# Which tiles of a softmax sum VectorE adds, and where the maxima stand: one edit to an attention kernel

## The reference, cut to what matters

```
h = layernorm(x) * (1 + ca) + sa                       # 2 x 2048 x 256
q, k, v = split_heads(h @ W + b)                       # 16 heads of 64
pattern = einsum('bhid,bhjd->bhij', k, q) / sqrt(64)
prob = softmax(pattern, axis=-2)                       # over the 2048 rows i
out = einsum('bhis,bhid->bhsd', prob, v)
x = x + ga * (concat(out) @ Wo + bo)
```

## Time and profile before

| | |
|---|---|
| Median of 3 runs | 4717.73 us (4717.35 to 4722.87) |
| Profiled execution, its own time | 4722.76 us |
| Span in the trace | 4721.0 us |
| PE busy | 4368.3 us (93%) |
| DVE busy | 3253.8 us (69%) |
| POOL busy | 2907.6 us (62%) |
| ACT busy | 2169.1 us (46%) |
| Chain that ended last, by engine | POOL 53%, issue 21%, PE 12%, DVE 8%, ACT 4% |

### The profile page before, as it was taken

How to read it: one execution, slowest core, us unless ns; L and a number is a source line. 1 busy time by engine, 2 the same in 40 slices (tenths; PEclk the granted TensorE clock), 3 DMA queues, 4 the chain that set the end, 5 groups by cost and what they waited for, 6 DMA issues and landing times.

```text
span 4721.0 us, 67306 instructions
## 1 busy us (share of the span) xinstructions
PE 4368.3 (93%) x25496; PEld 2574.1 (55%) x25496; DVE 3253.8 (69%) x4370; ACT 2169.1 (46%) x3523; POOL 2907.6 (62%) x1269
## 2 busy tenths in 40 slices
PE   7999999999999999999999999759998896989898
PEld 5545454454454454554545544337676675767575
DVE  6777877878777877778777787455654545665455
ACT  5444444444444444444444444326565434556442
POOL 2867767667667677677676676526665334666332
PEclk8999999999999999999999999879999998999899
DMA  2000000000000000000000000100000000000001
GB/s 78 6 11 14 7 11 7 14 11 5 15 11 5 11 15 6 11 13 8 11 6 15 11 5 7 40 18 1 1 1 5 33 1 19 1 1 1 1 1 36
DMA packets 81402, 55.74 MB, mean 12 GB/s; under 512 B 48532, under 2 KB 71016, under 8 KB 81128
## 3 DMA queue, kind: packets, MB, share of 16 engines
q1 hardware_dynamic: 81128, 51.92, 4.1%
HBM read 30.66 MB, written 4.19 MB: 7 GB/s over the span
## 4 chain that ended last, share of the span: by engine, by line
POOL 53%; issue 21%; PE 12%; DVE 8%; ACT 4%; POOLq 1%; DMA 0%; DVEq 0%; SPq 0%; ACTq 0%
POOL accp L770 41%; POOL lp L792 4%; PE psum L1665 4%; POOL accp L766 3%; PE psum L1794 2%; POOL rnorm L782 2%; POOL qk_u L787 2%; PE psum L1807 2%; DVE ssq L1262 1%; ACT lp L974 1%; PE psum L1711 1%; ACT qk_sq L958 1%; DVE qk_w L1274 1%; POOL ug_l L820 1%; DVE lneg L1288 1%
## 5 line engine op out<-in xcount | busy, mean ns | idle before, releaser
L770 POOL TENSOR_TENSOR accp<-accp,prob 128x1024 f32<-128x1024 f32 x704 | 1766.9, 2510 | 492.5 <-ACT prob L928 414.0
L928 ACT ACTIVATE prob<-psum 128x1024 f32<-128x1024 f32 x1024 | 1020.0, 1024 | 1461.4 <-PE psum L1518 1383.6
L1159 DVE TENSOR_REDUCE mx<-psum 128x1 f32<-128x512 f32 x1984 | 1276.2, 684 | 347.2 <-PE psum L1485 298.0
L1530 PE MATMUL psum<-prob,vv 128*64 128x512 f32 x4096 | 993.2, 606 | 0.0
L1485 PE MATMUL psum<-kh,qh 64*128 64x512 f32 x2048 | 493.6, 471 | 56.1 <-DVE mx L1159 48.7
L1530 PEld LDWEIGHTS psum<-prob,vv 128*64 128x64 f32 x4096 | 248.7, 136 | 490.3 <-issue 427.3
L1485 PEld LDWEIGHTS psum<-kh,qh 64*128 64x128 f32 x2048 | 205.3, 185 | 522.6 <-DVE mx L1159 442.0
L792 POOL TENSOR_TENSOR lp<-lp,lrcp 128x1024 f32<-128x1024 f32 x128 | 297.9, 2327 | 238.0 <-DVE lrcp L1294 238.0
L1518 PE MATMUL psum<-nm,one 64*128 64x512 f32 x2048 | 428.7, 408 | 13.9 <-ACT prob L928 6.5
L1518 PE MATMUL psum<-qh,kh 64*128 64x512 f32 x2048 | 412.2, 391 | 0.0
L1518 PE MATMUL psum<-qh,kl 64*128 64x512 f32 x2048 | 412.1, 391 | 0.0
(11 more groups left out here) (197 smaller groups left out, 6942.3 us busy)
## 6 DMA issues: line engine op xcount, KB each, us to landing
kl<-kl SPq DMA_DIRECT2D x64, 256.0 KB, 3.8
wqk<-L_attn_Wq SPq DMA_DIRECT2D x64, 64.0 KB, 2.0
rot_l<-const_rot SPq DMA_DIRECT2D x2, 2048.0 KB, 9.3
out<-lpT SPq DMA_DIRECT2D x32, 128.0 KB, 1.7
wqkv_l<-L_ffn_wqkv SPq DMA_DIRECT2D x4, 768.0 KB, 10.7
w_l<-L_ffn_w SPq DMA_DIRECT2D x4, 618.0 KB
wqk<-L_attn_Wk SPq DMA_DIRECT2D x32, 64.0 KB, 2.0
wv_p<-L_attn_Wv SPq DMA_DIRECT2D x16, 128.0 KB, 2.2
```

What stands on the lines that cost most here:

```text
L770: pool.tensor_tensor(acc_p[cp][:], first[:], prob[kt % PRING][:], ALU.add).then_inc(pool_sum, 1)
L928: act.activation(prob[t % PRING][:], psum[:, S_BANK + 2 * (t % 2):S_BANK + 2 * (t % 2) + 2, :].rearrange("p a b -> p (a b)"), ACT.Exp, sca ...
L1159: dve.tensor_reduce(mx4[:, e, qt, c:c + 1], ps, AX_X, ALU.max).then_inc(ring_free, 1)
L1530: mm = pe.matmul(psum[j * DH:(j + 1) * DH, O_BANK, :], vv[:, kt, s * DH:(s + 1) * DH], prob[t % PRING][:, j * T:(j + 1) * T], start=(kt == ...
```

## The change

VectorE still adds three tiles of each half and GpSimd thirteen, but other ones: tiles 8, 10 and 12 of the first half, and 1, 3 and 10 of the second. The copy is gone: VectorE's first addition takes the first two tiles, so it has two instructions a half in place of three. The buffer of the first of the two tiles is released by that first addition (`dve_used`). GpSimd's order is derived from the tiles that are left. The weights of groups 11 and 12, right behind the middle sum, change from 0 and 2 to 2 and 3.

The couples of the groups become, in an odd head, 1,2,3,2,3,2,2,3,2,2,3,1,2,2,2,0, and in an even head 1,2,2,2,2,2,3,2,3,3,2,1,2,3,2,0.

```diff
-SUM_DVE = (3, 7, 11)
-SUM_POOL = tuple(k for k in range(KT) if k not in SUM_DVE)
+SUM_DVE = ((8, 10, 12), (1, 3, 10))
+SUM_POOL = tuple(tuple(k for k in range(KT) if k not in tiles) for tiles in SUM_DVE)
...
-POOL_SEQ = SUM_POOL[1:-1] + (JOIN,) + SUM_POOL[-1:]
-POOL_OPS = len(POOL_SEQ)
-DVE_OPS = len(SUM_DVE)
+POOL_SEQ = tuple(tiles[1:-1] + (JOIN,) + tiles[-1:] for tiles in SUM_POOL)
+POOL_OPS = len(POOL_SEQ[0])
+DVE_OPS = len(SUM_DVE[0]) - 1
...
-            weight[SUM0_GROUP + 1:SUM0_GROUP + 3] = [0, 2]
+            weight[SUM0_GROUP + 1:SUM0_GROUP + 3] = [2, 3]
...
+        def dve_used(cp, kt):
+
+            return max(SUM_DVE[cp].index(kt), 1)
...
-                    if kt in SUM_DVE:
-                        act.wait_ge(dve_sum, G * (CP * DVE_OPS) + OFF_DVE + cp * DVE_OPS + SUM_DVE.index(kt) + 1)
+                    if kt in SUM_DVE[cp % CP]:
+                        act.wait_ge(dve_sum, G * (CP * DVE_OPS) + OFF_DVE + cp * DVE_OPS + dve_used(cp % CP, kt))
...
-                kt = SUM_DVE[j]
-                dve.wait_ge(exp_done, G * STEPS + cp * KT + kt + 1)
-                if j:
-                    dve.wait_ge(dve_sum, G * (CP * DVE_OPS) + OFF_DVE + cp * DVE_OPS + j)
-                    dve.tensor_tensor(acc_d[cp][:], acc_d[cp][:], prob[kt % PRING][:], ALU.add).then_inc(dve_sum, 1)
-                else:
-                    dve.tensor_copy(acc_d[cp][:], prob[kt % PRING][:]).then_inc(dve_sum, 1)
+                tiles = SUM_DVE[cp]
+                dve.wait_ge(exp_done, G * STEPS + cp * KT + tiles[j] + 1)
+                left = prob[tiles[0] % PRING]
+                if j > 1:
+                    dve.wait_ge(dve_sum, G * (CP * DVE_OPS) + OFF_DVE + cp * DVE_OPS + j - 1)
+                    left = acc_d[cp]
+                dve.tensor_tensor(acc_d[cp][:], left[:], prob[tiles[j] % PRING][:], ALU.add).then_inc(dve_sum, 1)
...
-                            if kt in SUM_DVE:
-                                add_sum(G, cp, SUM_DVE.index(kt))
+                            if kt in SUM_DVE[cp][1:]:
+                                add_sum(G, cp, SUM_DVE[cp].index(kt))
```

More of the change, by code:

```diff
@@ L407, in adaln_block, with pool_used @@
         OFF_S, OFF_POOL, OFF_DVE, OFF_RING = STEPS, CP * POOL_OPS, CP * DVE_OPS, RING_PAIR
-        def pool_used(kt):
-            return 1 if kt == SUM_POOL[0] else POOL_SEQ.index(kt) + 1
+        def pool_used(cp, kt):
+            return 1 if kt == SUM_POOL[cp][0] else POOL_SEQ[cp].index(kt) + 1
+        def dve_used(cp, kt):
+            return max(SUM_DVE[cp].index(kt), 1)
         def phase_end(eng, phase):
@@ L760, in head_sums @@
                 for cp in range(CP):
-                    for i, kt in enumerate(POOL_SEQ):
+                    for i, kt in enumerate(POOL_SEQ[cp]):
                         n = G * (CP * POOL_OPS) + OFF_POOL + cp * POOL_OPS + i
@@ L768, in head_sums @@
                         pool.wait_ge(exp_done, G * STEPS + cp * KT + kt + 1)
-                        first = acc_p[cp] if i else prob[SUM_POOL[0] % PRING]
+                        first = acc_p[cp] if i else prob[SUM_POOL[cp][0] % PRING]
                         pool.tensor_tensor(acc_p[cp][:], first[:], prob[kt % PRING][:], ALU.add).then_inc(pool_sum, 1)
@@ L923, in exps @@
                     cp, kt = divmod(t - PRING, KT)
-                    if kt in SUM_DVE:
-                        act.wait_ge(dve_sum, G * (CP * DVE_OPS) + OFF_DVE + cp * DVE_OPS + SUM_DVE.index(kt) + 1)
+                    if kt in SUM_DVE[cp % CP]:
+                        act.wait_ge(dve_sum, G * (CP * DVE_OPS) + OFF_DVE + cp * DVE_OPS + dve_used(cp % CP, kt))
                     else:
-                        act.wait_ge(pool_sum, G * (CP * POOL_OPS) + OFF_POOL + cp * POOL_OPS + pool_used(kt))
+                        act.wait_ge(pool_sum, G * (CP * POOL_OPS) + OFF_POOL + cp * POOL_OPS + pool_used(cp % CP, kt))
                     act.activation(prob[t % PRING][:], psum[:, S_BANK + 2 * (t % 2):S_BANK + 2 * (t % 2) + 2, :].rearrange("p a b -> p (a b)"),
```

## The result

The changed kernel takes 4839.34 us (median of 4, 4835.14 to 4847.48), the kernel before, on the same chip, 4718.75: a ratio of 1.0256, interval [1.0238, 1.0274]. It is slower, as forecast, but by 121 us where 72 were worked out, and 4839 lies outside 4735 to 4825.

What follows compares the result with a forecast made beforehand. PE's own order of work was taken as the bound, others costing only where PE waits. Losses of 53.6 (16 odd heads) + 16.8 (14 even) + 2 (last head), together 72 us, gave 4790 us, 1.5% slower; range 4765 to 4815.

Steps and rivals of the forecast that it cites:

- Term 4: Addition of tile 12, step 6: odd heads tie with GpSimd's tile 14, 1.05 us (bounds 0 and 2.1); even heads about 5.45.
- Term 1: Step 5: exponential 12 waits for the addition of tiles 8 and 10; PE loses 1.55 us, step 5.9 odd, 6.4 even.
- Term 2: Step 9: exponential 21 waits for the addition of tiles 1 and 3; step 6.0 us in odd heads, 5.3 in even.
- Term 3: Behind the middle sum: maxima queue behind VectorE's backlog, PE waits 1.7 us, steps 10 and 11 together take 11.15.
- the batch change: Its even head already has two couples in groups 11 and 12: taken as 0, bounds -1.5 and 2.4.
- the last head: No maxima, ends on GpSimd with one instruction more behind step 20: 2 us lost, bounds 0 and 2.5.
- With every tie lost 4807: Forecast's total in us if every tie goes the bad way; with every tie won it gave 4773.
- Rival A: Faster: scores 14 and 23 behind the two released exponentials don't really wait; 4681 us, chance 0.13.
- Rival B: Nothing changes: GpSimd's chain sets the pace and keeps its 26 instructions a head; 4718 us, chance 0.04.
- Rival C: Less loss: PE's new waits let VectorE catch up, following ring waits vanish; 4730 to 4765 us, chance 0.12.
- Rival D: More loss: GpSimd's tile 15 ends late, exponential 19 waits for it, 1.5 us in 32 heads; 4838 us, chance 0.09.

## Why the prediction was wrong

**The direction and most of the mechanism were right.** PE's order sets the time, the removed instructions gave nothing back that shows in a step, and the places that wait are those that were named. What failed is the price of one wait, the tie of term 4, and of what the clock loses behind it. By terms:

- Term 1: scores 14 late, step 5 5.9 and 6.4 forecast; 6.14 and 6.47 measured, PE idle 1.48 for 1.55. Right.
- Term 2: step 9 6.0 and 5.3 forecast, 6.07 and 5.38 measured. The size is right. In even heads the cause is too (with neighbours the step is 4.36). In odd heads it isn't the released buffer alone: with neighbours the step stays at 6.06, and PE waits as long there with either set of tiles (0.95 and 0.96). In the timelines above (values 18 at 1196.07) the addition takes 2.20 beside GpSimd's, and the reductions queued behind it hold a couple for 0.95, at nearly the time at which the exponential's release comes. Two limits lie on one another, and the working saw one.
- Term 3: 11.15 for steps 10 and 11, 11.13 measured, PE idle 1.66 for 1.7. Right. With one couple in place of two there, the step takes 4.14 for 6.12.
- Term 4: "This is a tie … I take half, 1.05, with 0 and 2.1 as bounds." **This step failed.** The tie is lost in all 16 heads, by 0.11 to 0.13 us: in the head above GpSimd starts at 1179.99, VectorE's addition at 1180.11. It then costs 2.17 (step 6 in heads without a fall, 7.22 against 5.05 with the addition moved). A tie of two times that are the same in each head is no coin: it fell one way every time, and half its price was a value it could hardly have. 16 heads by 1.12 are 18 us.
- The clock. **The prediction put it at nothing, without a word on it.** It said "the reductions behind it are late and step 6 takes 2.1 more", as if PE ran on at full speed behind it. Fourteen falls by 1.4 are 20 us. The added stall in the kernel before shows that such a wait can bring falls by itself (2 to 12), the moved addition that they go with it (16 to 2).
- Even heads lost 1.4 in place of 1.2, the batch change 2.4 in place of 0 (its upper bound), the last head nothing in place of 2. These three together are 3 us.
- The rest, 0.5 us a head of the odd kind: 0.24 in step 5, where the exponential starts 2.77 behind the values and not 2.67, and the next one adds a little; 0.03 to 0.09 in most others. 8 us.

Together: 72 forecast + 18 + 20 + 3 + 8 = 121. "With every tie lost 4807" would have been 32 us short still; 20 of them are the clock's.

Two sums of the working are off by little. 70.0 less 66.59 is 3.41 and 77.3 less 76.01 is 1.29, where it took 3.35 and 1.2: that is 2 us of the differences above. In rival A, 70.0 less terms 1, 2 and 4 (1.55, 0.93 and 1.05) is 66.5 and not 66.15, which makes 4687 and not 4681.

**What the working overlooked.** The addition of tile 12 holds exponential 16 too (idle 3.87 in the timeline of ACT). That costs nothing here, since PE's couple waits longer. It shows that the list of who waits for each late addition was not complete.

**The rivals.** Rival A's total needed its condition at every place. Moving the additions ahead makes it true in steps 5 and 9 of odd heads (4.40 and 5.04) and the total still is 4753: the lock takes in even heads what the release gives. Rival B fell, GpSimd waited for exponentials even more than before (921.5 us for 747.1). Rival C fell: after a wait the next ring waits did not shrink (steps 7 and 8 take 4.38 and 4.37 in odd heads without a fall, 4.35 forecast). Rival D's number, 4838, is the one measured, but its mechanism isn't: in the whole changed profile 7 exponentials wait for GpSimd's additions, 8.9 us in all, and moving VectorE's addition, which leaves GpSimd's list alone, gives back 56 us. A right total by a wrong path is not a hit.

**The chip's lock.** The Trainium skill, SBUF — State Buffer, "Who interferes with whom", says that of a Vector instruction with two SBUF inputs and a GpSimd one reading SBUF the first to issue has the port and the other waits. The rows agree to some 0.15 us on both sides. VectorE, 0.12 late, starts 2.26 ahead of GpSimd's end and takes 3.35, where 2.26 + 1.23 would be 3.49. With VectorE first it takes 1.23, and GpSimd's 2.38 become 2.50 with 0.26 of VectorE's addition still to run. A matching rule didn't help with the sum, since the question was who is first.

**What stays open.** Why two of 15 odd heads have no fall, five of 15 with the added stall, and 11 of 16 with the weights back, where the same stall of 2.1 us follows the same one of 1.48. In the changed kernel the steps ahead of the stall differ by less than 0.05 us between heads with and without, so the wait alone doesn't decide; where in time it lies was not varied. Nor was the removed copy's own cost measured: every run that puts copies back also moves a release.

## What to carry to other kernels

When a reduction is merged to save an instruction, look at which buffers its input held and when they come free now: taking neighbouring tiles instead of tiles two apart was worth 98 us, the clock's falls included, and 76 with the couples dealt by a table, while no run shows a gain from the instruction saved. When two engines that exclude each other are due within a tenth of a microsecond, work out both outcomes and give each a chance; don't average. And where a new stall of 2 us is forecast on PE, add what the clock may lose behind it, as a chance and not as a certainty.

## What the runs showed of the hardware

**A stall of PE of 2 us can cost more than itself.** In 13 of 15 odd heads the granted clock went from 1.00 to 0.5 behind a stall of 2.1 us that followed one of 1.48 in the step ahead, and each time some 1.4 us were lost beyond the stall. With the stall of 1.48 alone (tile 12 moved) there were 2 falls in all, as before the change. Counted over the runs, the clock fell behind 14 of 16 such stalls in the changed kernel, 5 of 16 with the weights back, 9 of 14 (1.89 us) with the copy kept, and 10 of 15 (2.0 us) with the stall added. Behind waits of 1.4 to 1.7 us it seldom did: none of 61 in the changed kernel, 2 of 14 in the one with neighbours and the weights back. The Trainium skill, TensorE: Matmul & The Clock Gate, "A second HAM failure mode: psum-queue depth-cycling", tells of a kernel whose clock goes down and up where PE idles briefly and often between groups as it cycles through PSUM banks; the trace agrees in kind, with the numbers above.

**The waiting side carries the lock's whole cost, and it may be either.** With VectorE waiting, GpSimd's addition takes 2.38 as ever and VectorE's 3.35. Where VectorE's was under way, GpSimd's takes 2.50 with 0.26 us of it left (tile 12 moved) and 3.18 with 0.93 left (changed kernel): the wait, less some 0.13.
